# Queries of batches 2 to 7 turned through DRAM and VectorE instead of TensorE, with their transfers ahead of context rows and weights

## What is computed

```python
q = layernorm(x)                                   # per row
scores = einsum('bqd,bkd->bqk', q, ctx) / sqrt(512)
p = softmax(where(mask, -1e9, scores))
atted = swapaxes(einsum('bqk,bkd->bqd', p, ctx), -1, -2)
x = x + einsum('bdl,ol->bdo', atted, W_merge) + b_merge
y = layernorm(x)
xq = fake_quant(y)                 # one scale from max|y| over everything
h = fake_quant(silu(xq @ fq(w_gate).T) * (xq @ fq(w_up).T))
out = x + h @ fq(w_down).T         # fq: per-row scale, rounded to int8
```

## Time and profile before

| | |
|---|---|
| runs | 544.58 us (543.73 to 544.82) |
| the profiled execution | 543.5 us, its span 541.7 us |
| TensorE matmul | 528.9 us busy, 98% |
| VectorE | 436.7 us, 81% |
| ScalarE | 298.4 us, 55% |
| GpSimd | 150.1 us, 28% |
| DMA queue q1 | 93.21 MB, 61.1% of 16 engines |
| granted TensorE clock | 1.000 |

### The profile page before, as it was taken

The page is one execution under the profiler, slowest core; times in us unless marked ns, Lnnn a source line. Parts: engine busy times, 40 slices in busy tenths (PEclk is TensorE's granted clock), DMA queues, the critical chain, the costliest instruction groups (busy, mean ns, idle before and its releaser), DMA issues. The chain is left out here.

```text
span 541.7 us, 7377 instructions
## 1 busy us (share of the span) xinstructions
PE 528.9 (98%) x2468; PEld 346.6 (64%) x2468; DVE 436.7 (81%) x806; ACT 298.4 (55%) x446; POOL 150.1 (28%) x100
## 2 busy tenths in 40 slices
PE   7899999999999999999999999999999999999996
PEld 6777888888888888888887444444444444344442
DVE  5787999979799698896767587778878777699984
ACT  4775774757547575575240645554554543976610
POOL 3369455755457553674031000000000000000000
PEclk9999999999999999999999999999999999999999
DMA  8925579685875857843476539658301102779874
GB/s 271 302 63 133 179 180 160 230 191 176 200 126 205 201 170 194 140 157 90 119 62 185 220 47 326 219 169 276 106 10 39 39 1 71 298 291 390 271 252 155
DMA packets 77600, 93.61 MB, mean 173 GB/s; under 512 B 36096, under 2 KB 54528, under 8 KB 75008
## 3 DMA queue, kind: packets, MB, share of 16 engines
q1 hardware_dynamic: 77568, 93.21, 61.1%
HBM read 59.77 MB, written 25.43 MB: 157 GB/s over the span
## 5 line engine op out<-in xcount | busy, mean ns | idle before, releaser
L1292 PE MATMUL gu<-hid,gu_T 128*128 128x512 f16 x704 | 152.1, 379 | 0.0
L1292 PEld LDWEIGHTS gu<-hid,gu_T 128*128 128x128 f16 x704 | 68.8, 98 | 83.2 <-DVE hid L1202 0.4
L1100 ACT ACTIVATE hid<-gu,gu_mul 128x512 f32<-128x512 f32 x88 | 59.6, 685 | 73.5 <-PE gu L1292 68.0
L1183 DVE SCALAR_TENSOR_TENSOR hid<-gu,gu_mul,hid 128x512 f32 (+1 forms) x88 | 65.0, 746 | 32.4 <-PE gu L1292 28.4
L1335 PE MATMUL gu<-wd_T,gu_T 128*128 128x512 f16 x264 | 58.0, 379 | 1.1 <-DVE gu_T L1231 0.8
L834 PE MATMUL mm<-wm_hi,p_hi 128*128 128x512 f32 x128 | 52.5, 410 | 1.9 <-DVE wm_lo L552 1.9
L1191 DVE TENSOR_REDUCE hmax<-hid 128x1 f32 (+2 forms) x48 | 53.2, 1119 | 0.7 <-DVE hid L1183 0.7
L834 PE MATMUL mm<-cT_hi,qT_hi 128*128 128x512 f32 x128 | 50.5, 395 | 0.7 <-DVE cT_lo L546 0.7
L1129 ACT ACTIVATE h<-hid,inv 128x1024 int8<-128x1024 f32 (+3 forms) x31 | 43.5, 1479 | 13.4 <-DVE gu_T L1231 13.4
L836 PE MATMUL mm<-wm_hi,p_lo 128*128 128x512 f32 x128 | 50.2, 392 | 0.0
L835 PE MATMUL mm<-wm_lo,p_hi 128*128 128x512 f32 x128 | 50.0, 391 | 0.0
(11 more groups left out here) (142 smaller groups left out, 923.2 us busy)
## 6 DMA issues: line engine op xcount, KB each, us to landing
h_dram<-hid SPq DMA_DIRECT2D x3, 2816.0 KB, 9.3
hid<-h_dram SPq DMA_DIRECT2D x3, 2816.0 KB, 11.9
cb<-in_ctx_dram SPq DMA_DIRECT2D x28, 256.0 KB, 7.8
cx<-in_ctx_dram SPq DMA_DIRECT2D x7, 1024.0 KB, 10.3
x<-in_x_dram SPq DMA_DIRECT2D x5, 1024.0 KB, 5.7
x_dram<-x SPq DMA_DIRECT2D x20, 256.0 KB, 2.4
xq<-x_dram SPq DMA_DIRECT2D x5, 1024.0 KB, 10.4
x<-x_dram SPq DMA_DIRECT2D x5, 1024.0 KB, 4.8
```

The lines of the kernel that those rows point to most:

```text
L1100: nc.scalar.activation(silu[SILU_AT[i]], gu[2 * (i % 3)][:], ACT.Silu, scale=gu_mul[:, 0, i:i + 1]).then_inc(silu_done, 1)
L1183: nc.vector.scalar_tensor_tensor(hid[:, b % SLOTS, i * L:(i + 1) * L], gu[2 * (i % 3) + 1][:], gu_mul[:, 1, i:i + 1], silu[SILU_AT[i]], AL ...
L1292: last = nc.tensor.matmul(gu[2 * (i % 3) + g][:], gu_T[:, g, h, i * P:(i + 1) * P], xT[p][:, h, :], start=h == 0, stop=h == T - 1)
```

## The change

1. **Queries.** `transposes`, `transposed_hi`, `transposed_lo` of batches 2 to 7 go. Instead `norm1` writes `qn` in plain order; SyncE stores the four tiles to `q_dram` (`move_q`), waits until they have landed, and fetches them back in 512 B blocks into `qb` with four transfers; VectorE turns `qb` (`turn_q`, four instructions, behind `mixed_lo(n, 0)`); ScalarE makes `qT_hi` (`query_hi`, four) and GpSimd `qT_lo` (`query_lo`, four).
2. **Queue order.** SyncE now does: `turn_w(n-1)`, `load_mask(n+1)`, `move_q(n+1)`, `load_c(n)`, `store_x1(n-1, 0)`, `load_w(n)`, the other three stores, `load_x(n+2)`, `load_cb(n+2)`. Context rows and weights of batch n are issued behind the queries of batch n+1.
3. **Probabilities** of batches 1 to 7 stay in the freed PSUM banks `tr`.
4. **Weights.** `weights16` moves from VectorE to ScalarE, right behind `weights_round(n)` and thus ahead of `exps(n+1, 0)`; the int8 and float16 forms lie inside `wst`.
5. **ScalarE's order.** `norm1(n+1)` comes behind `exps(n, 2)` and `exps(n, 3)`, two of the four masks behind `exps(n, 0)` and `exps(n, 1)`; `query_hi` stands ahead of `mixed_hi(n, 1)`, `context_hi(n)` ahead of `mixed_hi(n, 2)`. On VectorE `weights_scale(n)` stands behind `mixed_lo(n, 1)`, and `row_stats1` one tile earlier.
6. **Small ones.** `make_rstd1` ahead of `add_bias`; `make_c_lo` in four parts; `make_rstd2` and `variances2` of batches 0 to 6 once, as 128x28, at the end; the load of `d_scale` moves to the second block.

```diff
+                    def move_q(n):
+                        for t in range(T):
+                            sp.wait_ge(q_ready, T * n + t + 1)
+                            if n > 2 and t == 0:
+                                sp.wait_ge(q_moved, 64 * (n - 2))
+                            sp.dma_start(q_dram[t * P:(t + 1) * P, :], qn[:, t, :]).then_inc(q_stored, 16)
+                        sp.wait_ge(q_stored, 64 * (n - 1))
+                        if n > 2:
+                            sp.wait_ge(qT_ready, T * (n - 2))
+                        pieces = q_dram.rearrange("(t k j) (a f) -> a j t k f", j=BLK, k=P // BLK, f=P)
+                        for a in range(P // BLK):
+                            sp.dma_start(qb[a * BLK:(a + 1) * BLK, :, :].rearrange("j t (k f) -> j t k f", f=P),
+                                         pieces[a]).then_inc(q_moved, 16)
...
                         if n:
+                            if n < B - 1:
+                                move_q(n + 1)
+                            sp.wait_ge(c_ready, T * n)
+                            load_c(n)
+                            store_x1(n - 1, 0)
                             sp.wait_ge(w_done, through(n - 1, w_turns))
                             load_w(n)
-                            for t in range(T):
+                            for t in range(1, T):
                                 store_x1(n - 1, t)
...
-                        if n < B - 1:
-                            sp.wait_ge(c_ready, n + 1)
-                            load_c(n + 1)
...
+                    def query_lo(n):
+                        for t in range(T):
+                            gp.wait_ge(qT_hid, T * (n - 2) + t + 1)
+                            nc.gpsimd.tensor_tensor(columns(qT_lo, t), blocks(qb[:, t, :]), columns(qT_hi, t).bitcast(F32),
+                                                    ALU.subtract).then_inc(qT_ready, 1)
...
-                    make_rstd2(B - 1)
+                    make_rstd2(0, B - 1)
+                    make_rstd2(B - 1, B)
...
+                    def query_hi(n, t):
+                        act.wait_ge(qb_turned, T * (n - 2) + t + 1)
+                        if t == 0:
+                            act.wait_ge(s_done, T * n)
+                        nc.scalar.activation(columns(qT_hi, t), blocks(qb[:, t, :]), ACT.Copy).then_inc(qT_hid, 1)
...
+                    def weights16(n):
+                        act.wait_ge(w_rounded, through(n, rounds))
...
-                            elif t:
-                                probs_hi(n, t - 1)
+                            else:
+                                if t < 2:
+                                    make_mneg(n, t + 2)
+                                if t:
+                                    probs_hi(n, t - 1)
+                                if t >= 2 and not last:
+                                    norm1(n + 1, 2 * t - 4)
+                                    norm1(n + 1, 2 * t - 3)
...
                         for k in range(T):
+                            if k == 1 and not (start or last):
+                                for t in range(T):
+                                    query_hi(n + 1, t)
+                            elif k == 2 and not (start or last):
+                                context_hi(n)
+                            mixed_hi(n, k)
...
                         weights_round(n)
+                        weights16(n)
...
+                    def turn_q(n, t):
+                        if t == 0:
+                            dve.wait_ge(q_moved, 64 * (n - 1))
+                        nc.vector.transpose(qb[:, t, :], qb[:, t, :]).then_inc(qb_turned, 1)
...
-                        dve.wait_ge(rstd2_made, B - 1)
+                        dve.wait_ge(rstd2_made, 1)
...
                         for k in range(T):
+                            if k == 1 and not (start or last):
+                                for t in range(T):
+                                    turn_q(n + 1, t)
+                            elif k == 2 and not (start or last):
+                                weights_scale(n)
...
                     def scores(n, k):
                         if n:
                             pe.wait_ge(g_ready, T * (n - 1) + k + 1)
-                        pe.wait_ge(t_lo, turns(n, T + k) if n else max(turns(0, T + k), turns(0, T - 1)))
+                        if n > 1:
+                            pe.wait_ge(qT_ready, T * (n - 2) + k + 1)
+                        else:
+                            pe.wait_ge(t_lo, turns(n, T + k) if n else max(turns(0, T + k), turns(0, T - 1)))
...
-                                if not last:
-                                    transposes(n + 1, T + k)
                                 mixed(n, k)
```

More of the change, by code:

```diff
@@ L724, in _ @@
                         last, start = n == B - 1, n == 0
-                        if not start:
-                            weights16(n - 1)
                         for t in range(T):
@@ L745, in _ @@
                                     transposed_lo(0, T + 2 + t)
-                            elif t:
-                                invert_sum(n, t - 1)
-                                if t < 3 and not last:
-                                    row_stats1(n + 1, 2 * t - 2, 2 * t)
+                            else:
+                                if t:
+                                    invert_sum(n, t - 1)
+                                if t < 2 and not last:
+                                    row_stats1(n + 1, 2 * t, 2 * t + 2)
+                                if t == 2 and not last:
+                                    row_bias1(n + 1)
                                 if t == 3 and not last:
@@ L771, in _ @@
                                 row_min2(n - 1, k)
-                        weights_scale(n)
+                        if start or last:
+                            weights_scale(n)
                         for k in range(T):
+                            if k == 1 and not (start or last):
+                                for t in range(T):
+                                    turn_q(n + 1, t)
+                            elif k == 2 and not (start or last):
+                                weights_scale(n)
                             if start:
@@ L778, in _ @@
                             else:
-                                if not last:
-                                    transposed_lo(n + 1, T + k)
                                 mixed_lo(n, k)
@@ L786, in _ @@
                                 aggregate2(n - 1, k)
-                            variances2(n - 1)
-                    weights16(B - 1)
+                            if last:
+                                variances2(0, B - 1)
                     early_distances()
@@ L815, in transposes @@
                             pe.wait_ge(q_ready, T * n + g - T + 1)
-                            if n > 1:
-                                pe.wait_ge(t_lo, turns(n - 1, g))
-                            elif n == 0 and g == 2 * T - 1:
+                            if n == 0 and g == 2 * T - 1:
                                 pe.wait_ge(t_lo, turns(n, 0))
@@ L955, in ffn @@
                 d_mul = sb("d_mul", [P, D], F32)
+                d_scale = sb("d_scale", [P, D], F32)
+                scale_in = sem("scale_in")
                 spare = sb("spare", [P, 1], F32)
```

126 lines of the change are left out of this document (72 added, 54 removed).

## The result

The changed kernel takes 560.66 us (median of 4 runs, 555.97 to 561.76), the kernel before 544.7: ratio 1.0286, 95% interval 1.0256 to 1.0316. Predicted were 560.0; the 0.7 us between are less than the runs differ among themselves. The profiled execution took 559.89 us, its span is 557.7 us, 16.0 more than before.

What follows compares the result with a forecast made beforehand. TensorE (98% busy) was taken as the bound before; a longer loop over SyncE was to cover the work saved: 543.5 + 15.2 (attention stage) + 1.6 (end) = 560.3 us profiled, 561 as median, stated as 560.0, range 543 to 570.

Steps and rivals of the forecast that it cites:

- The bound of before and what goes: Attention stage: TensorE sets the 34.54 us period; without transposes 32.64, at most 11.4 us gained over batches 2 to 7.
- The loop over SyncE, odd n: Fetch to next fetch through weights, scaling, rounding, cast, transposes and query stores on SyncE's queue: 38.2 us.
- `turn_w` ... 8.6; the mask 0.9; four stores 3.0 and landing 0.7: Last SyncE steps of the odd loop: weight transposes, mask load, query stores and their landing, in us.
- ScalarE's way to `norm1` is a little shorter here: Odd loop: ScalarE's path to the norms was taken as slightly shorter than SyncE's and given no size.
- Even n: Fetch to next fetch in even batches: two ways join, 35 us by the weights and 35.8 by `x`.
- The pair: Odd and even loops together 74.0 us against 69.1 before: +4.9 per pair, +14.7 for three pairs.
- Where the idle time lies: TensorE was to idle 3 to 5 us ahead of `scores(n, 2)`, released by `g_lo`.
- The fetch's rate: Query fetch of a megabyte in 512 B blocks: 185 GB/s, taken as 5.2 us after 1.0 to start.
- rival 2: Query fetch runs at row rate, 2.3 us less per batch: 546 us; chance 0.07 together with another rival.
- Already by this sum the DMA engines are full: Added stores and fetch bring DMA time per batch to 33 to 36 us within TensorE's 32.64.
- The end: End of attention stage: one power of 28 columns, 4.6 us, delays the last residual by 1.6 us (0.2 to 4).
- Rival 1: TensorE stays the bound, all loops fit in 32.64 us, needing 9.4 less per pair: 534.8 us; chance 0.13.

Runs made afterwards that it cites:

- fetch_once: Changed kernel with the query fetch only for batch 2, later fetches and their waits left out, so later batches use old queries: 535.77 us.
- before_extra: Kernel before plus, per batch 1 to 6, four 256 KB stores and four 256 KB block fetches that nobody waits for: 544.0 us, ratio 1.0001.
- power_each: Changed kernel with the powers of 4 columns taken in every batch again instead of one of 28 columns at the end: 558.11 us.
- fetch_at_once: Changed kernel with the block fetch taken from context in DRAM, without SyncE's wait for the query stores to land: 547.41 us.
- down_late: Changed kernel with w_down's transposes behind the x1 stores (own float16 buffer), context rows first, weights directly behind the fetch, powers per batch: 550.36 us.
- gap_filled: Changed kernel with ten matmuls that nobody reads ahead of scores(n, 0) of n = 3, 5 and 7: 561.28 us.

## Why the prediction was right, point by point

**The bound of before and what goes.** Right. `fetch_once` shows 32.64 us as TensorE's own period with all the rest of the change in place.

**The loop over SyncE, odd n.** Forecast 38.2 us from fetch to fetch, measured 40.3 (137.07 to 177.38); the two others have 40.4 and 38.8. Fetch to the start of `gu_amax` 15.1 (forecast 16.1), scaling 3.2 (3.15), rounding 2.7 (2.6), cast 2.35 (2.3: ScalarE's own row was the right neighbour), and from there to the landed stores 16.9, where the sum had 14.0. The step that failed is "`turn_w` ... 8.6; the mask 0.9; four stores 3.0 and landing 0.7". SyncE is through with transposes and mask at 166.34 and then waits: the first store goes out at 167.48, when its norm is made. So the transposes' place in the queue was not on the path, and no row shows the 6.0 us for which that of `w_down` was to hold the queue; SyncE issued it in 1.5 to 4.0 us before and in 2.4 to 4.6 after. What was on the path is what the forecast had set aside with "ScalarE's way to `norm1` is a little shorter here". By way of `x`: 17.0 to its issue, 6.0 to its landing (160.06, only 0.4 ahead of the end of the cast), 11.3 to the last store, 6.0 to its landing; together 40.3. In the forecast's own terms this way was 18.25 + 5.5 + 10.6 + 3.3 = 37.7. It failed by the landing, 6.0 where 0.7 were counted; against that stand 2.6 less for the stores, which go out while the norms are made, and 1.3 less to the issue of `x`.

**Even n.** Forecast 35.8 by way of `x`, measured 34.9 (102.15 to 137.07): to the issue of `x` 16.1 (16.4), its landing 5.8 (5.5), statistics, masks, exponents and norms 11.3 (10.6), landing of the stores 1.7, where 3.3 for the stores were counted: they are issued while the norms run, and only the last one's landing is left.

**The pair.** 75.3 and 74.7 between fetches, forecast 74.0; the errors of the two halves, +2.1 and −0.9, cancel in part, and at the last batches and the start two more do. That the total came out within 0.7 us is luck; that it would be slower by a loop over the round trip is not. At TensorE the pairs cost +6.2 (batches 2, 3) and +4.9 (4, 5), batches 6 and 7 +5.8 together, the start and batch 1 −2.9; forecast were 4.9 each, 2 more for the last, −1.5 for the first: 15.2 against 14.1.

**Where the idle time lies.** Half right. `scores(n, 2)` waits for `g_lo` as forecast, but 1.3 to 2.2 us instead of 3 to 5, and the larger part in every second batch stands ahead of `scores(n, 0)` for `qT_lo`. The same loop closes at two of its members; I had followed it only through the weights.

**The fetch's rate.** Forecast 1.0 to start and 5.2 from the earlier trace rows. A piece lands in 4.9 (median); where VectorE waits for all four, it goes on 7.4 to 9.0 us after the first issue (9.0 from 137.07 to 146.06). The trace so goes on disagreeing with what the Trainium skill says (DMA: Bandwidth & Descriptors, Specifications) of 512 B as enough for line rate; rival 2 did not come about. That the 512 B and not the strided order makes the price, no run separates.

**"Already by this sum the DMA engines are full".** Wrong as a statement of capacity: `before_extra` moves the same bytes in 34.54 us for nothing. It is the time to landing behind other transfers that counts, not the sum.

**The end.** Right. 0.15 per column gave 4.6 us for 28 columns, measured 4.81; +1.6 forecast, +1.6 measured. With four columns at a time the 1.6 us are gone from the trace of `power_each`.

**A sum.** Rival 1 needs 74.0 − 2 × 32.64 = 8.7 us less per pair, not 9.4; nothing hangs on it.

**Not foreseen.** The late landing in odd batches, and the fall of the granted clock behind gaps. What the clock costs is open, as said above.

## What to carry to other kernels

When work leaves the bounding engine for a round trip through DRAM, write down the loop from one use to the next with every transfer that the engines still have in hand when the store is issued, not only with what is in the queue ahead: a transfer moved from behind the fetch to ahead of the store came back as a later landing. Test the gain by taking the wait out (`fetch_once`, `fetch_at_once`) before shuffling the order; it showed within two runs that 25 us hung on the round trip and 13 of them on one wait. Count transfers as well as bytes: sixteen small ones held the queue for 11 us. And compare all batches, from the last producer on: counted from the last store alone, `down_late` looks like a cure of the late landing, which it is not.

## What the runs showed of the hardware

- A 256 KB store of queries, issued 4 to 10 us behind the last transpose of an odd batch, with a 512-byte store of 4-byte values ahead of them, has landed 5.1 to 6.4 us after its norm, against 2.0 to 2.1 in even batches; in between the engines are 71% busy at 10 GB/s. A second queue does not help (5.7 to 6.6). Which transfer is to blame is open: taking the transpose of `w_down` away did not help (`down_late`).
- Right behind such a 512-byte store a megabyte load took 13.0 us to land (before, issued at 275.93), against 5.3 us elsewhere. The small store itself lands 14.1 us after its issue (after, median).
- SyncE issues one DMA transpose of a 128x1408 float16 tile in 1.5 to 4.6 us (before and after); it lands in 9.6 (after, median).
- A transfer of 64 KB from SBUF to SBUF costs 0.64 to 0.72 us of issue on SyncE, against 0.48 for a 256 KB piece from DRAM.
- GpSimd's power takes 1.02 us for 4 columns and 4.81 for 28.
- The length of a gap alone does not tell whether the granted clock falls. In after it was 0.50 behind 3.38 us of idle time (ahead of 187.58) and behind 2.17 (230.65), but 1.00 behind 3.23 (112.60). In `down_late` it fell behind each of 3.59, 4.27 and 4.02 us. In `gap_filled` it stayed at 1.00 behind the filled gaps, of which 2.40, 0.55 and 0.71 us were left idle, and fell where nothing was filled, with 2.58 us idle ahead of 157.28.
